# Four graph blocks on one core: the last projection group split around the first scores, and the sums of three blocks ended on VectorE

## The reference

```python
def _gat_layer(x, W, adj):                    # block 0: two such layers
    proj = x @ W
    Wh, Ws = jnp.split(proj, 2, axis=-1)
    scores = Wh @ Ws.T
    a = jax.nn.softmax(scores, axis=-1) * adj
    return jax.nn.leaky_relu(a @ Wh + x, 0.01)

# block 1
A_ = A + jnp.eye(n); d = jax.lax.rsqrt(A_.sum(axis=1))
relu(((A_ * d[:, None] * d[None, :]) @ H) @ W)
# block 2
deg = jnp.sum(adj, axis=1, keepdims=True) + 1e-05
relu(((adj / deg) @ h) @ W_neigh.T + b_neigh + h @ W_self.T + b_self)
# block 3
h = relu(adj @ (x @ W1) + b1)
adj @ (h @ W2) + b2
```

## Time and profile before

| | us |
|---|---|
| median of three runs (751.42 to 752.29) | 752.12 |
| the profiled execution | 751.27 |
| its span, first to last instruction | 749.5 |

### The profile page before, as it was taken

One profiled execution on the slowest core, in us unless ns is written; L12 is line 12 of the kernel. 1 busy time (PEld: TensorE's weight loads), 2 busy tenths in 40 slices (PEclk: granted clock), 3 DMA queues, 4 the chain that ended last, 5 costly groups with the idle time before them and its releaser, 6 DMA issues.

```text
span 749.5 us, 13371 instructions
## 1 busy us (share of the span) xinstructions
PE 720.8 (96%) x3962; PEld 610.6 (81%) x3962; DVE 476.0 (64%) x1083; ACT 347.6 (46%) x805; POOL 344.4 (46%) x377
## 2 busy tenths in 40 slices
PE   6989999999999998999999999989999999899996
PEld 5868888888888887888888888877877777689985
DVE  3567777777777655565665764763677746764356
ACT  3666656565665455455465475451223422332212
POOL 1046767677675414636445445484664001115500
PEclk9999999999999999999999999999999999999998
DMA  6043242423322211533232132245762221210012
GB/s 210 1 171 140 84 169 84 160 91 122 130 94 104 83 71 58 114 111 127 71 102 108 70 122 88 80 102 129 184 174 86 71 63 57 65 49 2 1 43 73
DMA packets 63138, 72.38 MB, mean 97 GB/s; under 512 B 36336, under 2 KB 56432, under 8 KB 58992
## 3 DMA queue, kind: packets, MB, share of 16 engines
q1 hardware_dynamic: 63088, 71.78, 30.1%
HBM read 46.60 MB, written 16.78 MB: 85 GB/s over the span
## 4 chain that ended last, share of the span: by engine, by line
PE 86%; DVE 5%; issue 3%; ACT 2%; POOL 2%; DMA 1%; SPq 0%; DVEq 0%; POOLq 0%; ACTq 0%
PE scores L1826 38%; PE ob L1826 27%; PE tb L1826 9%; PE tb L1954 7%; PE xb L1826 2%; POOL prob L668 1%; PE tb L1930 1%; DVE zb L1603 1%; DVE norm_values L1609 1%; DMA keep<-in_x 0%; PE tb L1845 0%; DVE zb L1547 0%; PE xb L1868 0%; ACT prob L872 0%; PE xb L1979 0%
## 5 line engine op out<-in xcount | busy, mean ns | idle before, releaser
L668 POOL TENSOR_TENSOR prob<-prob,arow 128x512 f32<-128x512 f32 x128 | 193.2, 1531 | 158.3 <-ACT prob L872 158.2
L1826 PE MATMUL ob<-val,stationary 128*128 128x512 f32 x960 | 186.5, 344 | 0.0
L1826 PEld LDWEIGHTS ob<-val,stationary 128*128 128x128 f32 x960 | 146.7, 189 | 18.3
L1189 DVE TENSOR_TENSOR stationary<-tb,stationary 128x512 fp32r<-128x512 f32 x128 | 85.5, 687 | 60.1 <-ACT stationary L772 58.9
L1826 PE MATMUL scores<-wst_h,whs_h 128*128 128x512 f32 x256 | 103.1, 403 | 4.0 <-ACT prob L872 4.0
L1826 PE MATMUL scores<-wst_h,whs_l 128*128 128x512 f32 x256 | 100.5, 393 | 0.0
L1826 PE MATMUL scores<-wst_l,whs_h 128*128 128x512 f32 x256 | 100.2, 391 | 0.0
L1294 DVE TENSOR_REDUCE row_values<-scores 128x1 f32<-128x512 f32 x128 | 85.8, 682 | 16.2 <-PE scores L1826 14.4
L772 ACT ACTIVATE stationary<-tb 128x512 fp32r<-128x512 f32 x128 | 73.0, 594 | 43.3 <-PE tb L1954 41.9
L872 ACT ACTIVATE prob<-scores,row_values 128x512 f32<-128x512 f32 x128 | 86.6, 689 | 4.8 <-DVE row_values L1301 4.8
L1954 PE MATMUL tb<-ident,prob 128*128 128x128 f32 x512 | 72.7, 273 | 2.1 <-POOL prob L668 1.8
(11 more groups left out here) (200 smaller groups left out, 1194.2 us busy)
## 6 DMA issues: line engine op xcount, KB each, us to landing
arow<-in_adj SPq DMA_DIRECT2D x32, 1024.0 KB, 4.9
adjacency_halves<-arow SPq DMA_DIRECT2D x16, 512.0 KB, 2.9
features_scratch<-xs SPq DMA_DIRECT2D x32, 128.0 KB, 1.9
xres<-features_scratch SPq DMA_DIRECT2D x32, 128.0 KB, 2.1
keep<-in_x SPq DMA_DIRECT2D x4, 512.0 KB, 6.2
xres<-in_x SPq DMA_DIRECT2D x16, 128.0 KB, 2.0
self_term_scratch<-rst SPq DMA_DIRECT2D x16, 128.0 KB, 1.7
rin<-self_term_scratch SPq DMA_DIRECT2D x16, 128.0 KB, 2.2
```

What stands on the lines that cost most here:

```text
L668: nc.gpsimd.tensor_tensor(prob[u][:, cs], prob[u][:, cs], arow[u][:, cs], ALU.mult).then_inc(g.msk.sem, 1)
L1189: return nc.vector.tensor_tensor(dst, v, h.bitcast(F32), ALU.subtract)
L1826: return nc.tensor.matmul(o, l, r, start=start, stop=stop)
```

## The change

In both attention layers the last projection group is cut into three. The keys come first, into the banks `ob0` and `xb0` that the attention products use later; then (in layer 0 behind the transposes of the later blocks' weights) all four score chunks of tile 0; then the queries in the same two banks, score chunk 0 of tile 1, and the values. For that the staging area moves from `prob[0]` to `prob[1]` and raw weights from `arow[0]` to `arow[1]`, and the adjacency row of tile 0 is loaded at the start. Its conversion and comparison stand between projection groups; tile 1's conversion stands behind the exponentials of tile 1. In layer 1 the flag's matmul moves behind `slot(0, 1)`, and the square root with its table ahead of the last keys.

In blocks 1 to 3 `halves` replaces `total`: VectorE adds the first half to the self loop (scaled ahead by ScalarE), the self term or the bias, and then the second half, both from PSUM. ScalarE's copy and GpSimd's two additions go. In block 3 ScalarE writes the rectified high part straight to `pm` and VectorE its low part, tile by tile, and TensorE waits for each tile.

```diff
@@ TensorE, start of a layer @@
-                project(NCH - 1)
-                score(0, 0, 0)
-                values(NCH - 1, 0)
-                values(NCH - 1, 1)
-                for c in range(1, NCH):
-                    score(0, 0, c)
-                ge(pe, g.vl, 2 * NCH + 1)
-                slot(0, 1, fin=False, norm=False)
+                last_keys()
+                if not l:
+                    weights()
+                for c in range(NCH):
+                    score(0, 0, c)
+                last_queries()
+                slot(0, 1, fin=False, norm=False, first=True)
@@ TensorE, slot @@
                     if main:
                         score(b, u, 0)
+                    if first:
+                        last_values()
+                        ge(pe, g.vl, 2 * (NCH - 1) + 1)
...
+                def last_keys():
...
+                    project_part(NCH - 1, KT, ob0)
+                    project_part(NCH - 1, KT + 1, xb0)
+
+                def last_queries():
+
+                    ge(pe, g.wsl, KT * NCH + 1)
+                    project_part(NCH - 1, 0, ob0)
+                    project_part(NCH - 1, 1, xb0)
@@ ScalarE, slot @@
                     if norm:
                         n_moving(b + u - 4, u)
+                    if first:
+                        cast_halves(b, u)
@@ ScalarE, start of a layer @@
+                group(0)
                 cast_halves(0, 0)
+                group(1)
...
-                slot(0, 0, av=False, fin=False, norm=False)
-                slot(0, 1, fin=False, norm=False)
...
+                slot(0, 1, fin=False, norm=False, first=True)
@@ VectorE, start of a layer @@
+                    degree(0, 0)
+                    compare(0, 0)
+                group(NCH - 2)
...
@@ VectorE, blocks 1 to 3 (C is block 1, Dg block 2, E and F block 3) @@
+                def halves(b, u):
...
+                    first, second = bank(b, u)[:, 0:w], bank(b, u)[:, w:2 * w]
...
+                    scale = (dinv if a is C else rdeg)[:, t:t + 1]
+                    nc.vector.scalar_tensor_tensor(zb[u][:, :], first, scale, rin[u][:, :],
+                                                   ALU.mult, ALU.add).then_inc(s_half, 1)
+                    dve.wait_ge(s_half, NT * k + t + 1)
+                    nc.vector.scalar_tensor_tensor(zb[u][:, :], second, scale, zb[u][:, :],
+                                                   ALU.mult, ALU.add).then_inc(a.r.sem, 1)
...
+            def hidden_lo(t):
+
+                dve.wait_ge(F.ph, t + 1)
+                nc.vector.scalar_tensor_tensor(pm[:, t, HID:2 * HID], zb[t % 2][:, 0:HID], 0.0,
+                                               pm[:, t, 0:HID].bitcast(F32), ALU.max, ALU.subtract)\
+                    .then_inc(E.new.sem, 1)
```

More of the change, by code:

```diff
@@ L819, in layer, with query_copy, key_hi @@
                 act.sem_inc(g.kept.sem, 1)
+                def query_copy(i, o, first, bank):
+                    ge(act, g.kept, i + 1)
+                    ge(act, g.prod, 4 * i + first + o + 2)
+                    copy(wht_g[:, o, :], bank[:, :]).then_inc(g.staged.sem, 1)
+                def key_hi(i, o, first, bank):
+                    ge(act, g.prod, 4 * i + first + o + 2)
+                    if not isinstance(i, int):
+                        alone(act, passed["scalar"])
+                    copy(wst_h[:, o, bass.ts(i, CH)], bank[:, :]).then_inc(g.wsh.sem, 1)
@@ new lines, in value_hi @@
+                def value_hi(i, h, bank):
+                    if l and h == 0:
+                        ge(act, G[l - 1].av, 4 * (NT - 1) + i + 1)
+                        if not isinstance(i, int):
+                            alone(act, passed["scalar"])
+                    ge(act, g.vt, 2 * i + h + 1)
+                    if not isinstance(i, int):
+                        alone(act, passed["scalar"])
+                    copy(val[:, bass.ds(i * TPC + 2 * h, 2), 0:D],
+                         bank[:, :].rearrange("p (a d) -> p a d", a=2)).then_inc(g.vh.sem, 1)
@@ L821, in group @@
                 def group(i):
-                    ge(act, g.kept, i + 1)
                     for o in range(KT):
-                        ge(act, g.prod, 4 * i + o + 2)
-                        copy(wht_g[:, o, :], scores[:, o * CH:(o + 1) * CH]).then_inc(g.staged.sem, 1)
+                        query_copy(i, o, 0, scores[:, o * CH:(o + 1) * CH])
                     if not l and i in (1, 2):
                         features(i + 1)
-                    if not l and i == 3:
-                        weights()
@@ L848, in layer @@
[L848 to L856, removed]
+                        key_hi(i, o, KT, scores[:, (KT + o) * CH:(KT + o + 1) * CH])
+                    for h in range(2):
+                        value_hi(i, h, tb[h])
@@ L1141, in exact @@
                         continue
-                    lo_half(0, 0)
+                    if a is E:
+                        for t in range(NT):
+                            hidden_hi(t)
+                        continue
+                    if a is C:
+                        self_scaled(0, 0)
                     deviation(0, 0)
@@ L1251, in group, with value_lo @@
+                def value_lo(i, h, bank):
+                    ge(dve, g.vh, 2 * i + h + 1)
+                    two = bass.ds(i * TPC + 2 * h, 2)
+                    rest(val[:, two, D:2 * D], bank[:, :].rearrange("p (a d) -> p a d", a=2),
+                         val[:, two, 0:D]).then_inc(g.vl.sem, 1)
+                def group(i):
+                    query_kept(i)
                     if not l and i in (1, 2):
                         features(i + 1)
-                    if not l and i == 3:
-                        weights()
@@ L1775, in exact @@
                         continue
+                    if a is E:
+                        for t in range(NT):
+                            total(t // 2 * 2, t % 2)
+                            if t:
+                                hidden_lo(t - 1)
+                        hidden_lo(NT - 1)
+                        continue
                     slot(0, 1, fin=False)
@@ L1981, in rows, with slot @@
                         last.then_inc(g.xtr.sem, 1)
-                def slot(b, u, main=True, av=True, fin=True, norm=True, last=False):
+                def slot(b, u, main=True, av=True, fin=True, norm=True, last=False, first=False):
                     p = before(b, u)
```

323 lines of the change are left out of this document (167 added, 156 removed).

## The result

| | median us | range | runs |
|---|---|---|---|
| before | 752.37 | 751.42 to 754.44 | 6 |
| after | 749.18 | 747.82 to 751.91 | 6 |

What follows compares the result with a forecast made beforehand. TensorE, busy 96% of the span, was taken as the bound, so only its waits counted. Terms -1.9, +2.9 and +1.5 gave 2.5 us: 751.27 to 748.8, 749.6 with 0.85 added back; range 745.0 to 752.4.

Steps and rivals of the forecast that it cites:

- The front of layer 0: Start of layer 0: the second score of tile 1 starts at 48.0 instead of 52.78, 4.8 us earlier.
- The rebound: Layer 0's first rows: tile 2's late conversion makes TensorE stand 5 us, giving back all 4.8 and 0.2 more.
- The clock behind it: After layer 0's 5 us pause: TensorE's granted clock falls, costing 1.7 us, bounds 0 and 2.5.
- Layer 0 together: All of layer 0: 4.8 won, 5.0 lost waiting and 1.7 lost by the clock, -1.9 us.
- Layer 1: Start of layer 1: second score of tile 1 at 288.3 instead of 291.42, no conversions to rebound, +2.9 us.
- Part 2: Blocks 1 to 3: sums ended by VectorE and hidden rows written per tile save 1.5 us together.
- Block 1's first tile: First rows of block 1: TensorE's wait of 0.45 at 523.87 saved, +0.4 us.
- Later tiles of block 2: Block 2 after its first tile: 0.1 at each of four waits, +0.4 us, bounds -1.6 and +1.6.
- no fall: Rival, layer 0: the clock does not fall in the pause, 1.7 better, 747.9 us; chance 0.17.
- no rebound: Rival, layer 0: conversion, store and load are covered, so no pause, 742.9 us; chance 0.11.
- second pause: Rival, layer 0: tile 3's conversion is late too and another 5 us is paid, 754.6 us; chance 0.10.
- VectorE did not become the bound of every tile of block 2: Rival, block 2: VectorE sets all 16 tiles, 1.6 lost, 751.6 us; chance 0.14 shared with a longer pause.

Runs made afterwards that it cites:

- the run that filled it: The changed kernel plus 20 matmuls with unread results on TensorE, right ahead of the wait at layer 0's first rows: 748.12 us, ratio 0.9941.
- Putting the half back: The changed kernel with layer 0 in its old order, tile 0's conversion and comparison staying in the projection: 745.93 us, ratio 0.9915.
- the early conversion: The changed kernel with tile 1's adjacency conversion moved ahead, behind the first two copies of tile 0's transposed weights: 741.64 us, ratio 0.9857.
- the conversion moved: The kernel before with only tile 1's adjacency conversion moved back, behind tile 1's last exponential: ratio 1.0071, 5.3 us slower.
- part 2 alone: The kernel before with only blocks 1 to 3 changed (sums ended by VectorE from PSUM, hidden rows written tile by tile): 749.93 us, ratio 0.9962.

## Why the prediction was right, step by step

The terms -1.9, +2.9 and +1.5 gave a gain of 2.5 us; in the traces they are -3.05, +3.0 and +1.9, so 1.8, and the medians moved by 3.2 to 3.5. In both layers the mechanisms came as forecast, each with its place and its releaser; in the blocks a part of the gain came from elsewhere. That the median is met to 0.4 us is in part luck: in the traces layer 0 came out worse than its term and the blocks better.

- The front of layer 0, 4.8 earlier: 4.6 measured.
- The rebound, all given back and 0.2 more: 0.5 more, by the load, which took until 66.07 instead of 65.6. The wait of 5.0, its place and its releaser came as computed; moving the conversion in either kernel takes the pause away or makes it.
- The clock behind it, 1.7: a term of the right mechanism that was sized too small in this trace, 2.5, since about 5 us ran at the lower level and I took the 3.4 us that followed the shorter wait. The step's upper bound of 2.5 was reached. The rule of the Trainium skill, "TensorE: Matmul & The Clock Gate", Part 1, that activity lifts the half rate and an idle engine falls back, agrees with the pause of 5 us and with the run that filled it (0.57 against 1.00).
- Layer 0 together -1.9: -3.05 in the trace. Putting the half back is worth 2.9 to 3.3, in a kernel whose layer 0 is also 1.2 faster than before by the early comparison. I had costed that at nothing by itself; the row for it stood there, the first four masks taking 7.08 beside the comparison.
- Layer 1, +2.9: 3.0.
- Part 2, +1.5: 1.9 in the trace, 2.4 by the medians alone. Block 1's first tile gave 0.34 for 0.4, though TensorE's wait at its rows did not go: it is 0.26 for 0.45. Of the 1.1 from block 1's first rows to block 2's, 0.3 was won at the later projections of block 1 (0.13 ahead at its first rows, 0.43 ahead at 595.71), which I had left at nothing, and 0.8 at block 2's first tile, for 0.7. Later tiles of block 2 gave 0.56 for 0.4: the four waits fell from 3.1 to 1.9, and 0.8 came back as two waits of 0.4 for the low part of the rows on VectorE, which has one instruction more per tile.
- The rivals: "no fall" did not come in the trace, "no rebound" was priced 742.9 and is what the early conversion gives, 741.6; no second pause followed, and VectorE did not become the bound of every tile of block 2.

That the median moved by 3.2 and the profiled execution by 1.4 is within the spread of single executions. Not settled is how often the clock falls behind a given pause. The six executions of the changed kernel all have a mean clock of 0.993 and those with the early conversion 0.996 to 0.998, which speaks for a fall in each of the six, though only one of them was traced.

## What to carry to other kernels

When work is moved to the front, look for whatever else of the next stage hangs behind the same point in each engine's order: here a conversion for later blocks, put behind one more tile's exponentials, held a single buffer through a store and a comparison and ate all of the 4.6 us that the front had won. A gain at a start is real only if the next wait downstream comes earlier as well, so follow the chain with the trace's own durations as far as the next place where the engine waited or just did not. And put side work where its engine is idle and does not slow the work that the slowest engine waits for: here that was worth 1.2 us in the trace.

## What the runs showed of the hardware

The clock does not answer the same wait in the same way. In the kernel before, 1.88 us of idleness in layer 0 brought the clock to 0.57 over 48 to 52, and 2.15 us in layer 1 left it at 1.00. With the conversion moved in that same kernel, the same 1.88 us left it at 1.00, and with part 2 alone the same 2.15 us brought it to 0.70 and 0.50:

```profile
48.00:52.00 4.00, 1.45 (x11) 1.07 (x10) 3.44 (x4) 1.26 (x3) 4.00 (x3) 1.00 0.00 0
```
```profile
288.00:290.00 2.00, 2.00 (x9) 1.53 (x8) 0.23 (x1) 1.59 (x6) 2.00 (x2) 0.70 0.00 0
290.00:292.00 2.00, 2.00 (x9) 1.76 (x8) 1.16 (x2) 1.12 (x2) 2.00 (x3) 0.50 0.00 0
```

A longer wait behind it, for the masks, differs too: 2.55 us with the conversion moved brought the clock to 0.71 and 0.50, and 2.57 us with part 2 alone left it at 1.00:

```profile
51.66 0.66 PE L1978 MATMUL tb<-ident,prob 128*128 128x128 f32 x4 [2.57 <-POOL prob L667]
52.07 0.48 PE L1850 MATMUL scores<-wst_h,whs_h 128*128 128x512 f32 x1
```
```profile
48.00:56.00 8.00, 5.43 (x28) 4.35 (x27) 5.39 (x7) 4.05 (x10) 7.19 (x6) 1.00 0.24 77
```

A step that rests on such a fall should carry both values. Behind the pauses of 3.7 to 5 us the clock fell in each trace that was read.

A fall need not cost time either. In the kernel before, tile 1 goes from its first score at 47.75 to its second at 52.78 in 5.03 us, at the lower clock; with part 2 alone it goes from 47.02 to 52.07, in 5.05, at full clock. The masks set the length of that stretch in both, and the slower matmuls only filled the wait for them (1.28 for 2.57). So what a slow stretch costs depends on whether a wait stands behind it; behind the pause of 5.0 none did.

GpSimd's four masks took 7.08 us with the comparison beside them and 5.49 with it elsewhere:

```profile
44.27 5.49 POOL L668 TENSOR_TENSOR prob<-prob,arow 128x512 f32<-128x512 f32 x4 [23.26 <-ACT prob L872]
```

The loss is not spread over the four. In the kernel before, one mask starts while the comparison runs (48.85 to 51.18) and takes 3.32, 2.0 more than the others' 1.3; the comparison itself takes 2.33 there, about the 2.29 that it takes alone. At 61.01 it is the comparison that starts second, while a mask runs to 62.10, and it takes 3.23, 0.9 more:

```profile
48.99 3.32 POOL L668 TENSOR_TENSOR prob<-prob,arow 128x512 f32<-128x512 f32 x1
```
```profile
60.81 1.29 POOL L668 TENSOR_TENSOR prob<-prob,arow 128x512 f32<-128x512 f32 x1 [0.48 <-ACT prob L872]
```

In both places the one that started second took longer by about the time that the other still had to run. The Trainium skill, "SBUF — State Buffer", "Who interferes with whom", says that a VectorE instruction with two inputs in SBUF contends with a GpSimd instruction that reads SBUF; these durations agree.
